# A decoder layer on one core: new SBUF places for the operands of TensorE

## The reference

```
x = x + attn(layernorm(x))       # 32 query heads, 8 key heads of 128; 16 blocks of 32 cached
                                 # positions picked by an index, and 128 new ones; no mask
x = x + xattn(layernorm(x))      # inside: rmsnorm * weight for the queries; 32 heads of 128;
                                 # keys and values from ctx (8, 128, 512); position bias, mask
x = x + ffn(layernorm(x))        # gelu(x W1 + b1) W2, nan and inf to 0, + b2; width 2048
```

## Time and profile before

| | |
|---|---|
| median of three runs | 2099.35 us |
| the profiled execution | 2101.18 us, its span 2099.2 us |
| PE busy | 2049.7 us, 98% |
| DVE, ACT, POOL busy | 1480.2, 1017.4, 530.9 us |
| mean granted clock of TensorE | 0.995 of full speed |

### The profile page before, as it was taken

How to read it: one execution, slowest core, us unless ns; L and a number is a source line. 1 busy time by engine, 2 the same in 40 slices (tenths; PEclk the granted TensorE clock), 3 DMA queues, 4 the chain that set the end, 5 groups by cost and what they waited for, 6 DMA issues and landing times.

```text
span 2099.2 us, 33914 instructions
## 1 busy us (share of the span) xinstructions
PE 2049.7 (98%) x11620; PEld 1779.2 (85%) x11620; DVE 1480.2 (71%) x2365; ACT 1017.4 (48%) x2232; POOL 530.9 (25%) x428
## 2 busy tenths in 40 slices
PE   8999999999999999999899999999999999989996
PEld 6888888888888888887788888888888888877885
DVE  6677777777777777777766666666666666677776
ACT  4555555555555555555544444444444444443331
POOL 3122122221222122222122222222222222223223
PEclk9999999999999999999999999999999999999998
DMA  7000000000000000011111111111111111010111
GB/s 237 16 21 16 16 21 20 20 11 19 20 20 15 15 20 20 15 46 41 47 44 43 42 43 42 42 38 37 37 41 42 42 42 42 23 36 26 50 46 50
DMA packets 44162, 76.90 MB, mean 37 GB/s; under 512 B 7378, under 2 KB 13650, under 8 KB 43602
## 3 DMA queue, kind: packets, MB, share of 16 engines
q1 hardware_dynamic: 43826, 74.15, 11.4%
q10 hardware_dynamic: 288, 2.10, 0.3%
HBM read 74.13 MB, written 2.10 MB: 36 GB/s over the span
## 4 chain that ended last, share of the span: by engine, by line
PE 93%; DVE 5%; ACT 1%; issue 1%; DMA 0%; SPq 0%; DVEq 0%; ACTq 0%
PE bank L1098 23%; PE bank L1100 23%; PE bank L1099 23%; PE bank L1172 11%; PE bank L1221 6%; PE bank L1289 1%; PE bank L1373 1%; PE bank L1290 1%; PE bank L1374 1%; PE bank L1348 1%; DVE xn L805 1%; DVE xT_lo L811 1%; DVE stats L773 0%; DVE xacc L887 0%; DVE kv_lo L831 0%
## 5 line engine op out<-in xcount | busy, mean ns | idle before, releaser
L887 DVE SCALAR_TENSOR_TENSOR xacc<-bank,rinv,xacc 128x512 f32<-128x512 f32 x512 | 375.9, 745 | 71.7 <-PE bank L1100 71.5
L484 ACT ACTIVATE pT_hi<-bank 128x512 fp32r<-128x512 f32 x320 | 190.9, 598 | 214.1 <-PE bank L1221 214.1
L877 DVE TENSOR_REDUCE negmax<-bank 128x1 f32<-128x640 f32 x256 | 210.1, 821 | 42.1 <-PE bank L1172 33.7
L923 DVE TENSOR_TENSOR pT_lo<-bank,pT_hi 128x512 fp32r<-128x512 f32 x320 | 217.4, 679 | 2.4 <-ACT pT_hi L484 2.4
L538 ACT ACTIVATE prob<-bank,negmax 128x640 f32<-128x640 f32 x256 | 202.7, 792 | 25.6 <-DVE negmax L877 25.6
L1221 PE MATMUL bank<-ident,prob 128*128 128x128 f32 x1280 | 191.2, 272 | 0.0
L1221 PEld LDWEIGHTS bank<-ident,prob 128*128 128x128 f32 x1280 | 159.1, 140 | 19.5
L381 POOL TENSOR_TENSOR wo_lo<-wo_raw,wo_hi 128x512 fp32r<-128x512 f32 x32 | 41.5, 1296 | 422.9 <-ACT wo_hi L484 422.9
L631 ACT ACTIVATE xprob<-xscore,negmax 128x128 f32<-128x128 f32 x256 | 99.4, 391 | 95.0 <-DVE negmax L974 95.0
L1098 PE MATMUL bank<-xwv_hi,cT_hi 128*128 128x256 f32 x512 | 141.7, 277 | 1.4 <-DVE xV_lo L941 1.4
L1100 PE MATMUL bank<-xwv_hi,cT_lo 128*128 128x256 f32 x512 | 141.5, 276 | 0.0
(11 more groups left out here) (171 smaller groups left out, 5792.2 us busy)
## 6 DMA issues: line engine op xcount, KB each, us to landing
wq_raw<-in_wq SPq DMA_DIRECT2D x32, 256.0 KB, 2.6
wo_raw<-in_wo SPq DMA_DIRECT2D x32, 256.0 KB, 2.6
xwv_raw<-in_xwv SPq DMA_DIRECT2D x16, 512.0 KB, 3.5
xwk_raw<-in_xwk SPq DMA_DIRECT2D x32, 256.0 KB, 3.7
xwq_raw<-in_xwq SPq DMA_DIRECT2D x32, 256.0 KB, 3.6
xwo_raw<-in_xwo SPq DMA_DIRECT2D x32, 256.0 KB, 2.7
w_raw<-in_w SPq DMA_DIRECT2D x32, 256.0 KB, 2.6
xacc<-in_x SPq DMA_DIRECT2D x8, 256.0 KB, 4.7
```

Of the source, the lines that this page charges most:

```text
L484: return s.activation(dst, src, ACT.Copy)
L877: v.tensor_reduce(negmax[:, slot, i:i + 1], S_bank[i % 2], mybir.AxisListType.XY, ALU.max, negate=True).then_inc(a["max"], 1)
L887: v.scalar_tensor_tensor(xacc[:, 4 * half + i, :], M, rinv[:, k, i:i + 1], xacc[:, 4 * half + i, :], ALU.mult, ALU.add).then_inc(sems["y"], 1)
L923: v.tensor_tensor(pT_lo[:, j, :], T_bank[j % 2 if k == 0 else (j + 1) % 2], pT_hi[:, j, :], ALU.subtract).then_inc(a["pTlo"], 1)
```

## The change

Tiles that nothing reads or writes are made larger or put in, so that those behind them in the stack move. No instruction, wait or transfer is changed, only the places in them. In bytes: `shift2` 32 to 352, `shift3` and `shift4` 32 to 480, new are `shift1` 448, `ahead3` 576, `ahead1` 64, `ahead2` 64, `back2` 384. The highest byte in use goes from 226,688 to 228,032.

```
-        sb(ctx, "shift2", [P, 8])
+        sb(ctx, "shift2", [P, 88])
...
             idx_sb = sb(ph, "idx_sb", [1, TOPK], I32)
+            sb(ph, "shift1", [P, 112])
             with ExitStack() as pro:
...
                 oT_hi, oT_lo = pair(lo_, "oT", [P, HALF])
+                sb(lo_, "ahead3", [P, 144])
                 xwv_raw = sb(lo_, "xwv_raw", [P, C, 2 * P])
...
             anykey = sb(ph, "anykey", [P, B])
-            sb(ph, "shift3", [P, 8])
+            sb(ph, "shift3", [P, 120])
             comb = sb(ph, "comb", [P, 2, 4, P])
             xq_hi, xq_lo = pair(ph, "xq", [P, 2, HALF])
+            sb(ph, "ahead1", [P, 16])
             xk = sb(ph, "xk", [P, 2, 4, 2, P], F32R)
...
                 xscore = sb(lo_, "xscore", [P, 2, 4, P])
+                sb(lo_, "ahead2", [P, 16])
                 xpT = sb(lo_, "xpT", [P, 4, 2, P], F32R)
+                sb(lo_, "back2", [P, 96])
                 xo = sb(lo_, "xo", [P, 2, 4, P])
...
             b1_sb = sb(ph, "b1_sb", [P, 2])
-            sb(ph, "shift4", [P, 8])
+            sb(ph, "shift4", [P, 120])
             b2_sb = sb(ph, "b2_sb", [P, D])
```

## The result

The changed kernel takes 2095.62 us (median of 17 runs, 2094.54 to 2097.33) against 2099.35 (17 runs): a ratio of 0.9982, 95% interval [0.9975, 0.9988]. It is 3.7 us faster where 20 were forecast. The profiled execution took 2096.01 us, its span is 2094.1. Lines behind L92 of the kernel stand up to 5 further down than before; L1103 to L1105 are the three passes of `mm3`.

The account below looks back on a forecast made before the run. PE, busy 98% of the span, was taken as the bound. Gains of 14.4 (512 columns) and 6.1 (256 columns) less 1.9 (transposes) made 18.6 us, hence 2080.8; 1.7 for easier entries gave 2079 us, range 2063 to 2098.

Parts of the forecast that it names:

- The last two stay at their price: `values` (distance 64) and self attention's K with q (0 and 256) keep their distances, so their passes cost the same.
- no-change rival: Whole kernel: price differences come from what runs around a group (history), not from places; 2099 us, chance 0.14.
- The cover is 235 and 280 us of DVE's idle time: Both attention loops: DVE's idle time, over ten times the gain, absorbs any wait a shorter PE step uncovers.
- 256-column passes, 6.1 us: Cross attention's score and sum passes, moved to distance 64, fall from 282 to 276 ns: 6.1 us gained.
- 512-column passes of cross attention, 7.1 us and 1.7 for easier entries: Queries, outputs and keys at distance 0 gain 7.1 us after settling costs; cheaper entries into these rows add 1.7.
- Self attention, 3.5 us: Output, `pv` and query passes at distance 0 gain 205 ns a step, less 150 for settling: 3.5 us.
- the sum for 512 columns: Self attention's 512-column passes: 55 ns a step left after settling, over 63 steps, 3.5 us gained.
- Transposes, 1.9 us lost: Self attention's transposes of prob, moved from 256 to 0, might lose 3.8 us; half was charged, 1.9.
- FFN, 3.8 us: Both FFN products at distance 0 gain 120 ns in each of 32 steps, without settling cost: 3.8 us.

Follow-up runs that it names:

- e2: Kernel before with the change's places in self attention and FFN, plus cross attention's query weights at distance 0; 2095.37 us, ratio 0.9973.
- p1: Only TensorE works, layer left out: blocks of 24 passes at eight distances behind different passes; 512 columns took 226.7 ns at distance 0, 233.3 at 192.
- p2: Only TensorE works, layer left out: cross attention's pass sequence without waits, 14 sets of places; four units took 53.58 us with the places before, 53.52 with the change's.
- e5: The changed kernel, with DVE adding the first output product to xacc ahead of the next scores' maxima in units without `values`; 2094.94 us, ratio 0.9975.
- e9: Kernel before with the change's places in self attention and FFN, and in cross attention only xpT moved, by 192 bytes; 2089.24 us, ratio 0.9945.

## Why the prediction was wrong

The direction was right (the interval lies below 1), though the 3.7 us are less than the 4.2 that the prediction took as the least to be told from nothing. The mechanism was right in half: the distance from stationary to moving operand bears on a pass's price, and at distance 0 rows of 512-column passes settle at 226.7 ns. That it alone sets the price was wrong, and the size by a factor of more than five. Step by step:

- **"The last two stay at their price"** is the step that failed. `values` keeps its distance and costs 6.5 us more. I took a price for a property of the distance, and had read its history only as a settling time of a few passes. e2 and p1 show that the same block at the same places has two steady prices, held for all its 24 passes, and p2 that the passes ahead choose. The no-change rival named history, but as all or nothing, and gave the evidence that should have made me ask: the queries of the two attentions have the same distance to xT and other means.
- **"The cover is 235 and 280 us of DVE's idle time."** A sum over the stage says nothing of one place. The row of DVE operations ahead of the second output product was full before; PE started there 0.13 us behind the end of DVE's addition. The shorter queries and output products run into it: +2.5 us. e5 shows a second such place right behind it.
- **256-column passes, 6.1 us.** 1.7 came. At distance 64 scores and sums ran near the dearer of the two prices (117.6 and 116.9 ns in the mean from pass to pass), like `values`. The price of `values` in the earlier trace rows was no promise for them. e9 gets 2.5 us from the sums alone, by a distance of 192.
- **512-column passes of cross attention, 7.1 us and 1.7 for easier entries.** 3.9 came, without the wait: 2.5 behind keys, 1.4 in the queries. Keys, which had distance 0 before, did not change, and the output product behind the scores gained 12 ns of 708.
- **Self attention, 3.5 us.** 6.3 came, and the surplus is luck. Output products, `pv` and queries gave 4.7, of it 1.5 by the clock at the stage's end, so 3.2 by the places: the sum for 512 columns held. The 320-column scores, which I left at their price, gave 1.8, though K and q moved together. Whether the passes ahead or the new places did that, no run separates.
- **Transposes, 1.9 us lost.** Nothing: 108.5 ns between them before, 108.6 after. By the period of 256 bytes that p1 shows, prob's move from 256 to 0 was no move at all. And it is the kind of pass, not the place, that makes the 112 ns of the warming products; in p1 128-column passes have 111.7 at every distance (all behind 512-column passes).
- **FFN, 3.8 us.** 3.6: where all passes have 512 columns, the distance alone was a sufficient model.

The rule of the Trainium skill that I set against the change ("TensorE: Matmul & The Clock Gate", Step-by-step: two independent read ports, loading weights takes no bandwidth from the running matmul; "SBUF — State Buffer", Who interferes with whom: PE never waits on anyone) would give p1 one price for all distances. It measured 226.7 to 233.3 ns for 512 columns and 113.3 to 120.0 for 256 with no other engine at work, so here the rule doesn't hold within PE itself. Between PE and the other engines nothing here speaks against it: p2, with PE alone, has the prices of the kernels. What stopped PE at the second output product was that DVE's result came late, and e5 removed it there.

What stays open. Why the clock falls behind the stops at the ends of the attention stages in some profiles and not in others. By the places the change has -4.8 us in self attention, +3.3 in the regular part of cross attention and -3.6 in the FFN, together -5.1, and the medians say -3.7. At an equal mean clock of 0.994 twelve of the 53 runs of before, on other chips, took 2100.6 us in the mean and seven of the change 2095.8, 4.8 less; so the clock may be the difference, which is not shown. And how the passes ahead choose the price: the runs show that they do and that a stop of PE can, not by what state.

## What to carry to other kernels

Once PE is the bound, with passes like these (fp32r, a weight load for each), the place of a moving operand relative to its stationary one (modulo 256 bytes) is worth 1 to 3% of a 512-column pass and up to 6% of a 256-column one in p1, and it costs nothing to try. But forecast it by running the whole sequence of passes alone, not by a price per distance, and add the waits, which that sequence doesn't have. Look at the single blocks: a mean between two prices is a mix of both. Move one group at a time and read every group's mean, above all of those that did not move. Look for cover at the place of each wait: idle time summed over a stage is none. And look at the granted clock behind every long stop before you count a stage's gain.

## What the runs showed that I had not expected

- The period is 256 bytes: 512 columns 226.7, 228.9, 232.9, 233.3 ns at 0, 64, 128, 192, and 226.7, 228.9, 231.7, 233.3 at 256 to 448.
- 256 columns: 119.6 to 120.0 at distance 0 in each row tried, 113.3 or 117.8 at 64 and at 192, 118.8 to 120.0 at 128. 320 columns 146.4 to 146.7 and 128 columns 111.7 at all distances, each tried behind one kind of pass only.
- 512 columns have more than one price too: 228.9 at distance 64 in p1, but 230.0 (units with `values`) and 233.2 (units without) in the queries of the kernel before, at the same distance modulo 256.
- At distance 128, a steady row is a cycle of unequal distances (228 to 241 ns over seven passes, again and again), not one price.
